# A fused two-layer network on one core: single-precision products made from half-precision parts

## The reference

```python
attn_out = out @ Wo + bo
x = x + attn_out
x_norm2 = layer_norm(x, g2, beta2)
ffn = jax.nn.relu(x_norm2 @ W1 + b1) @ W2 + b2     # W1 256 x 1024, W2 1024 x 256
return x + ffn
```

## Time and profile before

| | us |
|---|---|
| median of 3 runs | 1931.04 (1930.85 to 1933.86) |
| the profiled execution | 1943.5 |
| its span, first to last instruction | 1941.8 |
| PE busy | 1676.4 (86%) |
| VectorE busy | 1316.1 (68%) |
| ScalarE busy | 1083.6 (56%) |
| mean granted clock of PE, share of 2.4 GHz | 0.921 |

### The profile page before, as it was taken

How to read it: one execution, slowest core, us unless ns; L and a number is a source line. 1 busy time by engine, 2 the same in 40 slices (tenths; PEclk the granted TensorE clock), 3 DMA queues, 4 the chain that set the end, 5 groups by cost and what they waited for, 6 DMA issues and landing times.

```text
span 1941.8 us, 34714 instructions
## 1 busy us (share of the span) xinstructions
PE 1676.4 (86%) x13900; PEld 913.9 (47%) x13900; DVE 1316.1 (68%) x2014; ACT 1083.6 (56%) x1942; POOL 276.1 (14%) x248
## 2 busy tenths in 40 slices
PE   6988868999798999846999999999999679886877
PEld 4556645666566888521333333333333433462252
DVE  4223343381276888659999999999991686427867
ACT  3312112888643888311999999999999106311620
POOL 3223001898320000300000000000000000000000
PEclk9989989999888999875999999999999779886978
DMA  8123110899723766266433533543400070118100
GB/s 321 66 87 94 32 44 20 279 282 298 228 96 107 240 237 200 69 100 93 84 60 74 99 65 63 91 84 60 83 25 2 19 98 3 44 35 106 39 1 22
DMA packets 144653, 196.62 MB, mean 101 GB/s; under 512 B 34454, under 2 KB 109864, under 8 KB 140232
## 3 DMA queue, kind: packets, MB, share of 16 engines
q1 hardware_dynamic: 142764, 190.07, 38.1%
q0 software_dynamic: 1728, 4.33, 0.7%
HBM read 143.04 MB, written 51.00 MB: 100 GB/s over the span
## 4 chain that ended last, share of the span: by engine, by line
PE 43%; DVE 41%; issue 5%; POOL 4%; DMA 3%; ACT 2%; SPq 1%; another core or an unknown queue 1%; DVEq 0%; ACTq 0%; POOLq 0%
DVE mx_part L2200 28%; PE bank L1192 5%; PE pair L1234 5%; DVE mx L2309 3%; POOL k_part L2541 2%; PE bank L1045 2%; PE bank L1336 2%; PE pair L1395 2%; PE bank L252 2%; PE pair L1160 2%; PE pair L1147 2%; PE bank L1089 2%; DMA xT<-x_slots 2%; POOL c_lo L2528 2%; PE pair L1551 2%
## 5 line engine op out<-in xcount | busy, mean ns | idle before, releaser
L1743 ACT ACTIVATE pexp_all<-bank 128x512 f32<-128x512 f32 x1024 | 551.9, 595 | 97.9 <-PE bank L1350 84.5
L2200 DVE TENSOR_REDUCE mx_part<-pair 128x2 f32<-128x1024 f32 x512 | 583.0, 1213 | 16.6 <-PE pair L1322 14.2
L1336 PE MATMUL bank<-pexp_all,vst 128*17 128x256 f32 x4096 | 321.4, 386 | 6.0 <-issue 6.0
L1322 PE MATMUL pair<-kst,qs 49*128 49x512 f16 x1024 | 210.0, 407 | 44.7 <-DVE mx_part L2200 28.0
L1350 PE MATMUL bank<-qs,kst 52*128 52x256 f16 x2048 | 203.2, 271 | 0.0
L1322 PEld LDWEIGHTS pair<-kst,qs 49*128 49x128 f16 x1024 | 50.4, 93 | 273.2 <-DVE mx_part L2200 215.0
L1350 PEld LDWEIGHTS bank<-qs,kst 52*128 52x128 f16 x2048 | 120.7, 95 | 57.0 <-ACT pexp_all L1743 18.4
L1760 ACT ACTIVATE pexp_all<-bank 128x512 f32<-128x512 f32 x128 | 67.6, 595 | 120.5 <-PE bank L1458 120.3
L1336 PEld LDWEIGHTS bank<-pexp_all,vst 128*17 128x17 f32 x4096 | 68.6, 95 | 114.7 <-issue 105.3
L1677 ACT ACTIVATE hid_f<-bank,b 128x256 f32<-128x256 f32 (+1 forms) x152 | 78.6, 519 | 51.1 <-PE bank L1192 36.0
L1234 PE MATMUL pair<-w_hi,hid_hi 128*128 128x256 f16 x368 | 101.1, 275 | 3.2 <-issue 1.8
(11 more groups left out here) (323 smaller groups left out, 3042.5 us busy)
## 6 DMA issues: line engine op xcount, KB each, us to landing
w_f<-in_w_all SPq DMA_DIRECT2D x34, 1024.0 KB, 6.2
kst<-k_scr SPq DMA_DIRECT2D x192, 128.0 KB
v_scr<-v_st SPq DMA_DIRECT2D x64, 272.0 KB, 3.3
vst<-v_scr SPq DMA_DIRECT2D x16, 1088.0 KB, 5.6
ctx_sb<-in_ctx SPq DMA_DIRECT2D x16, 1024.0 KB, 5.0
cT<-in_ctxT SPq DMA_DIRECT2D x32, 512.0 KB, 5.6
k_scr<-k_part SPq DMA_DIRECT2D x128, 128.0 KB, 3.6
x_slots<-zeros SPq DMA_DIRECT2D x1, 3840.0 KB, 21.1
```

Source lines behind the costliest of these rows:

```text
L1322: last = pe.matmul(pair[n % 2][:, e * 512:(e + 1) * 512], qs[g % NBK][rws, p, qt * P:(qt + 1) * P], kst[g % NBK][rws, p, kb * 512:(kb + 1) ...
L1336: last = pe.matmul(bank[3][32 * h:32 * h + HV, 0:S], vst[g % 2][:, c, h * HV:(h + 1) * HV], unit_exp[n % NUE][:, p * S:(p + 1) * S], start ...
L1743: act.activation(unit_exp[n % NUE], bank[SCORE_BANKS[n % 3]], ACT.Exp, scale=SCALE).then_inc(s_exp, 1)
L2200: dve.tensor_reduce(mx_part[:, :, 2 * p + qt, kb], pair[n % 2][:, :].rearrange("p (e k) -> p e k", e=2), X_AXIS, ALU.max).then_inc(s_mx, 1)
```

## The change

- The network's two weight matrices go into one tensor of 8 pieces of 512 columns, `r_f`, with a high and a low half, `r_part`. They are loaded in `self_io(sa5)` where the expert weights are loaded in `self_io(sa6)`, and the halves are made beside steps 16 to 31 of `sa5` by the code that does it for the expert weights in `sa6`.
- `turn5` writes each transposed block twice, as single precision and as its high half; VectorE subtracts for the low half (`inputs_low`).
- Each product of the network becomes three of half precision. ScalarE's Relu writes one of four slots of `h5_f` and waits for the slot; VectorE makes the two halves of it.
- The bias row is added to `x` beside `sa5`, `u` is added between the first hidden jobs in four parts, and the scale of 1024 is taken out in the Relu and in VectorE's last addition.

```diff
-            hid5 = sb("hid5", [P, HM, NTOK], F32, sc)
-            r_w1 = sb("r_w1", [P, KT, HID], F32, sc)
-            r_w2 = sb("r_w2", [P, HM, D], F32, sc)
...
-        turn5 = Turn(tok, [(xT, "L1_attn_g2", "L1_attn_beta2")])
+        turn5 = Turn(tok, [(xT, "L1_attn_g2", "L1_attn_beta2"), (x5_part[0], "L1_attn_g2", "L1_attn_beta2")])
...
                 for b in range(B):
                     max_rows(b)
+                    if b == 1 and sa.turn == 0:
+                        sp.dma_start(r_f[:, 0:KT * HID].rearrange("p (k n) -> p k n", k=KT),
+                                     a["r_w1"].rearrange("(k p) n -> p k n", p=P)).then_inc(s_wa, 16)
+                        sp.dma_start(r_f[:, KT * HID:8 * 512].rearrange("p (m n) -> p m n", m=HM),
+                                     a["r_w2"].rearrange("(k p) n -> p k n", p=P)).then_inc(s_wa, 16)
...
             self_io(sa5, self_scr[0])
-            sa5.wait(sp, "mx", SELF_RING)
-            sp.dma_start(r_w1[:, :, :], a["r_w1"].rearrange("(k p) n -> p k n", p=P)).then_inc(s_wa, 16)
-            sp.dma_start(r_w2[:, :, :], a["r_w2"].rearrange("(k p) n -> p k n", p=P)).then_inc(s_wa, 16)
...
             pe_turn(pe, turn5, tiles_ready(norm5))
-            pe.wait_ge(s_wa, 16 * 4)
+            pe.wait_ge(s_wlo, FIRST_PIECES + 8)
             job = 0
             for half in range(2):
-                turned(pe, turn5, half)
+                pe.wait_ge(s_xlo, FIRST_INPUTS + KT * (half + 1))
                 for m in range(HM):
                     if job >= 4:
                         pe.wait_ge(s_h5e, job - 3)
                     for k in range(KT):
-                        last = pe.matmul(bank[4 + job % 4], r_w1[:, k, m * P:(m + 1) * P],
-                                         xT[:, k, half * 512:(half + 1) * 512], start=(k == 0), stop=(k == KT - 1))
+                        for i, (w_, x_) in enumerate(((0, 0), (0, 1), (1, 0))):
+                            last = pe.matmul(bank[4 + job % 4], r_w1[w_][:, k, m * P:(m + 1) * P],
+                                             x5_part[x_][:, k, half * 512:(half + 1) * 512],
+                                             start=(k == 0 and i == 0), stop=(k == KT - 1 and i == 2))
                     last.then_inc(s_h5, 1)
                     job += 1
             for t in range(T):
-                pe.wait_ge(s_h5e, HM * (t // 4 + 1))
+                pe.wait_ge(s_hlo, FIRST_HIDDEN + HM * (t // 4 + 1))
                 if t >= 2:
                     pe.wait_ge(s_x, 4 * T + t - 1)
                 for m in range(HM):
-                    last = pe.matmul(bank[2 + t % 2][:, 0:D], hid5[:, m, t * P:(t + 1) * P], r_w2[:, m, :],
-                                     start=(m == 0), stop=(m == HM - 1))
+                    for i, (h_, w_) in enumerate(((0, 0), (0, 1), (1, 0))):
+                        last = pe.matmul(bank[2 + t % 2][:, 0:D], h5_part[h_][:, m, t * P:(t + 1) * P], r_w2[w_][:, m, :],
+                                         start=(m == 0 and i == 0), stop=(m == HM - 1 and i == 2))
                 last.then_inc(s_m2, 1)
...
             def self_exp(sa):
                 for n in range(2 * SELF_STEPS):
-                    if sa.turn == 1 and n >= 32 and n % 4 == 0:
-                        last_weights_high((n - 32) // 4)
+                    if n >= 32 and n % 4 == 0:
+                        tail_weights_high(sa.turn, (n - 32) // 4)
...
             for job in range(2 * HM):
-                half, m = divmod(job, HM)
                 act.wait_ge(s_h5, job + 1)
-                act.activation(hid5[:, m, half * 512:(half + 1) * 512], bank[4 + job % 4], ACT.Relu,
-                               bias=col("L1_attn_b1", m)).then_inc(s_h5e, 1)
+                if job >= 4:
+                    act.wait_ge(s_hlo, FIRST_HIDDEN + job - 3)
+                act.activation(h5_f[:, job % 4, :], bank[4 + job % 4], ACT.Relu, bias=col("L1_attn_b1", job % HM),
+                               scale=1.0 / W_SCALE).then_inc(s_h5e, 1)
...
+            def beside_second_pass(turn, n):
                 if n >= 17 and n % 2 == 1:
-                    last_weights_low((n - 17) // 2)
+                    tail_weights_low(turn, (n - 17) // 2)
                 if n in (18, 20, 22, 24):
                     i = (n - 18) // 2
                     ts = slice(2 * i, 2 * i + 2)
+                    if turn:
+                        st.link(dve.tensor_tensor(u[:, ts, :], u[:, ts, :], per_tile_rows("L1_ffn_be1", 2), ALU.add))
+                    st.link(dve.tensor_tensor(x[:, ts, :], x[:, ts, :],
+                                              per_tile_rows("L1_ffn_be2" if turn else "L1_attn_b2", 2), ALU.add))
...
             dve_norm(dve, st, norm5, u, tok, measured=True)
-            st.link(dve.tensor_tensor(x[:, :, :], x[:, :, :], u[:, :, :], ALU.add))
+            inputs_low(turn5, x5_part)
+            for job in range(2 * HM):
+                half, m = divmod(job, HM)
+                hs = slice(half * 512, (half + 1) * 512)
+                dve.wait_ge(s_h5e, job + 1)
+                st.link(dve.tensor_copy(h5_part[0][:, m, hs], h5_f[:, job % 4, :]))
+                st.settle()
+                dve.tensor_tensor(h5_part[1][:, m, hs], h5_f[:, job % 4, :], h5_part[0][:, m, hs], ALU.subtract)\
+                    .then_inc(s_hlo, 1)
+                if job in (0, 2, 4, 6):
+                    ts = slice(job, job + 2)
+                    st.link(dve.tensor_tensor(x[:, ts, :], x[:, ts, :], u[:, ts, :], ALU.add))
             st.settle()
-            st.link(dve.tensor_tensor(x[:, :, :], x[:, :, :], per_tile_rows("L1_attn_b2"), ALU.add))
-            st.settle()
             def add_mlp(t):
                 dve.wait_ge(s_m2, t + 1)
-                dve.tensor_tensor(x[:, t, :], x[:, t, :], bank[2 + t % 2][:, 0:D], ALU.add).then_inc(s_x, 1)
+                dve.scalar_tensor_tensor(out=x[:, t, :], in0=bank[2 + t % 2][:, 0:D], scalar=1.0 / W_SCALE, in1=x[:, t, :],
+                                         op0=ALU.mult, op1=ALU.add).then_inc(s_x, 1)
```

More of the change, by code:

```diff
@@ L593, in wait @@
                 eng.wait_ge(signals[what].s, self.turn * signals[what].each + n)
-        with ExitStack() as sc:
-            sa5 = SelfAttention(0, sc)
-            cosT = sb("cosT", [P, S], F32, sc)
-            sinT = sb("sinT", [P, S], F32, sc)
-            rot_a = [sb(f"rot_a{i}", [P, 512], F32, sc) for i in range(2)]
-            rot_b = [sb(f"rot_b{i}", [P, 512], F32, sc) for i in range(2)]
-        with ExitStack() as sc:
-            hid5 = sb("hid5", [P, HM, NTOK], F32, sc)
-            r_w1 = sb("r_w1", [P, KT, HID], F32, sc)
-            r_w2 = sb("r_w2", [P, HM, D], F32, sc)
+        with ExitStack() as weights:
+            r_f = sb("r_f", [P, 8 * 512], F32, weights)
+            r_part = [sb(f"r_{part}", [P, 8 * 512], F16, weights) for part in ("hi", "lo")]
+            with ExitStack() as sc:
+                sa5 = SelfAttention(0, sc)
+                cosT = sb("cosT", [P, S], F32, sc)
+                sinT = sb("sinT", [P, S], F32, sc)
+                rot_a = [sb(f"rot_a{i}", [P, 512], F32, sc) for i in range(2)]
+                rot_b = [sb(f"rot_b{i}", [P, 512], F32, sc) for i in range(2)]
+            with ExitStack() as sc:
+                h5_f = sb("h5_f", [P, 4, 512], F32, sc)
+                h5_part = [sb(f"h5_{part}", [P, HM, NTOK], F16, sc) for part in ("hi", "lo")]
+                x5_part = [sb(f"x5_{part}", [P, KT, NTOK], F16, sc) for part in ("hi", "lo")]
+        r_w1 = [w[:, 0:KT * HID].rearrange("p (k n) -> p k n", k=KT) for w in r_part]
+        r_w2 = [w[:, KT * HID:8 * 512].rearrange("p (m n) -> p m n", m=HM) for w in r_part]
         norm4a, norm4b, norm5 = Norm(), Norm(), Norm()
@@ L617, in build @@
             wg_l = sb("wg_l", [P, KT, ER], F32, sc)
[L618 to L619 removed]
+            l_f = sb("l_f", [P, 8 * 512], F32, sc)
+            l_8 = [sb(f"l_{part}", [P, 8 * 512], F16, sc) for part in ("hi", "lo")]
+            l_part = [w[:, :].rearrange("p (e k n) -> p e k n", e=ER // 2, k=KT) for w in l_8]
             x6_part = [sb(f"x6_{part}", [P, KT, NTOK], F16, sc) for part in ("hi", "lo")]
@@ L1745, in _, with tail_weights_high @@
             act_turn(act, turn3o)
-            def last_weights_high(i):
-                act.wait_ge(s_wa, 16 * 5)
-                e, k = divmod(i, KT)
-                act.activation(l_part[0][:, e, k, :], l_we[:, e, k, :], ACT.Copy, scale=W_SCALE).then_inc(s_whi, 1)
+            def tail_weights_high(turn, i):
+                act.wait_ge(s_wa, 16 * (5 if turn else 4))
+                f, hi = ((r_f, r_part[0]), (l_f, l_8[0]))[turn]
+                cs = slice(i * 512, (i + 1) * 512)
+                act.activation(hi[:, cs], f[:, cs], ACT.Copy, scale=W_SCALE).then_inc(s_whi, 1)
             def self_exp(sa):
                 for n in range(2 * SELF_STEPS):
-                    if sa.turn == 1 and n >= 32 and n % 4 == 0:
-                        last_weights_high((n - 32) // 4)
```

(25 more changed lines are left out.)

26 lines of the change are left out of this document (13 added, 13 removed).

## The result

The change makes the kernel faster. Median 1917.24 us (6 runs, 1905.37 to 1923.24), the kernel before 1931.51 us, timed beside it (6 runs, 1930.85 to 1933.86): ratio 0.9921, 95% interval 0.9894 to 0.9947. That is 14.3 us less, where 9.6 were forecast; 1917.24 lies 0.6 us under the forecast's range. The forecast is a ratio of 0.995, just outside this interval. All three lie on the same side of it, but by the times alone the miss is small; what shows it is the profiles, stage by stage.

The account below looks back on a forecast made before the run. The prediction took PE's unbroken chain through the two-layer network as the bound. Network -11.2 us and splitting +1.6 gave -9.6, from the median of 1931.04 to 1921.4 us; range 1917.8 to 1925.5.

Parts of the forecast that it names:

- The first layer: Network's first layer: 96 half-precision products replace 32 of single precision, 22.8 us instead of 28.38, partly at half clock.
- Its start: Transposes ahead of the first layer: two destinations per job make its products start 1.0 us later, at 1674.0.
- The second layer: Network's second layer: 192 half-precision products replace 64 of single precision, 20.97 us instead of 27.64.
- VectorE and ScalarE: Under the first layer: their work stays hidden, VectorE ending about 2 us after the layer, with 3 us of cover.
- The splitting: Second pass of the self-attention ahead of the network: making the weight halves costs 1.6 us, ends 0.8 and 2.4.
- the stage ends at 1717.8, where it ended at 1729.03: 11.2 us less: End of the network's second layer: 1696.8 plus 21.0 gives 1717.8, 11.2 us less, carried whole into the sum.
- The sum: Whole kernel: -11.2 + 1.6 = -9.6 us, from the median of 1931.04 to 1921.4.
- The range: Whole kernel: 1917.8 to 1925.5 us, with the first rival in it.
- VectorE as the bound: First rival, network: at 1.45 us per pair VectorE would be late by 3 us, for 1924.4; chance 0.05.
- Late weights: Second rival, attention ahead: loads land late and hold ScalarE's first cast; at 33 us landing 1930, no change; chance 0.04.
- the cover of 15 us: Attention ahead: weights in by 1613.5, next maxima rows issued at about 1615, first cast at 1629; moved loads cost nothing.
- The clock held down: Third rival, first layer: clock stays at 1.2 GHz, layer 41.0 us, kernel 8.6 us slower, 1939.6; chance 0.04.

Follow-up runs that it names:

- after_again: The changed kernel, unchanged, timed and profiled a second time: 1933.76 us against 1949.5 for the kernel before, ratio 0.9926.
- vector_extra: The changed kernel with the cast of each hidden job made twice on VectorE: PE waits 2.67 us, the network is 4.5 us longer.
- high_only: The changed kernel with only the product of the two high halves in both layers: network 30.6 us from first product to end of last.
- before: The kernel before the change, in its first profile: profiled execution 1943.5 us, median 1931.51 us.
- before_again: The kernel before, unchanged, timed against itself and profiled a second time: 1948.79 us against 1949.5, ratio 0.9995.
- split_only: The changed kernel's loads and splitting, but the network in single precision from the loaded weights as before: ratio 0.9999 to the kernel before.
- after_shift6: The changed kernel with six small products (1.3 us) ahead of the second layer: 333.9 us from the second pass of `sa5` to the end, against 327.2.
- after: The changed kernel in its first profile: profiled execution 1923.24 us, median 1917.24 us, ratio 0.9921 to the kernel before.
- after_third: The changed kernel, unchanged, timed and profiled a third time: 1938.17 us against 1949.57 for the kernel before, ratio 0.9931.
- late_load: The changed kernel with its two weight loads issued after the fourth batch's maxima rows instead of the second's: the pass takes 64.4 us instead of 50.5.
- before_shift11: The kernel before with eleven small products (2.35 us) between the layers: 341.13 us from `sa5`'s second pass to the end, 341.10 and 341.14 without.
- the two warmed ones: Both kernels with small products on PE ahead of three norms' transposes: changed 1931.82 us beside 1949.5 (0.9905), before 1924.44 beside 1929.06 (0.9977).

## Why the forecast was wrong, point by point

The direction and the main term were right. The time lay outside the range, by 0.6 us, because the step that adds up the stages took those behind the network as fixed, and one of them got shorter; a second, smaller part is the term of the splitting, which was too large.

**The first layer**: right. 22.77 us (22.8), products 0.215 us apart, the clock rising 4.2 us after the first (4.3). The reason given, holes in the transposes that keep the clock down longer, fits the profiles: here the clock falls 0.9 to 1.8 us ahead of the first transpose in both kernels, and half speed lasts 6.8 us in the four profiles with single precision and one destination and 10.2 us in the seven with two. The agreement to 0.03 us is partly luck: in after_again the layer took 22.42 us, since the clock had fallen 0.7 us earlier against the work.

**Its start**: right, 1.1 us later (1.0). **The second layer**: right, 20.97 us (20.97). **VectorE and ScalarE**: right. VectorE ended 1.9 us after the first layer (2), and vector_extra and high_only put the point of waiting and its size where the count had them. The network as a whole gave 11.4 us, forecast 11.2.

**The splitting**: the mechanism was right and the size was not. The step "from the exponentials at 1629.22 to the gathering ... from the cast at 1818.45" measured one stretch from the exponentials and the other from the cast ahead of them. That cast lies in idle time, so its 0.6 us were wrongly counted as cost; read from the same event the rows give 1.06. By the profiles it is 1.0 us to the gathering (1.6 forecast, ends 0.8 to 2.4). To the network's transposes it is 0.4 on average; that last 0.6 is where the clock falls in the pass and in the projection behind it, and no size of the splitting.

**What was missing**: "the stage ends at 1717.8, where it ended at 1729.03: 11.2 us less" took for granted that all behind it keeps its length. The same work behind the network runs 3.4 or 10.2 us at half speed, by where the fall of the clock lies against PE's transposes. The table has all profiles without added products ahead of the norm, worked out from windows of 0.2 us:

| profile | the clock falls, us ahead of the first transpose | half speed lasts | projection |
|---|---|---|---|
| before | 0.96 | 10.2 | 9.61 |
| before_again | 0.84 | 10.2 | 9.67 |
| split_only | 1.67 | 10.2 | 9.26 |
| after_shift6 | 1.73 | 10.2 | 9.23 |
| vector_extra | 1.10 | 10.2 | 9.54 |
| after | 0.03 | 3.4 | 7.34 |
| after_again | 0.38 | 3.4 | 7.34 |
| after_third | 0.03 | 3.4 | 7.34 |
| high_only | 0.31 | 3.4 | 7.34 |
| late_load | 0.14 | 3.4 | 7.34 |
| before_shift11 | 0.10 inside them | 3.4 | 7.34 |

The fall itself comes 3 to 4.8 us after PE's last product of the network. PE then stands idle up to the transposes; between them and the projection it idles another 0.7 us. In the kernel before the clock had fallen 0.96 us ahead of the transposes and came back only in the projection. In the changed one it fell 0.03 us ahead of them and came back at 1719.77, inside the last transposes. That gave 2.3 us in the projection and 2.5 with the transposes. The remaining 0.3 of the 2.8 us up to the maxima is not clock but the balance of two others: SyncE's ten issues of that chain took 1.4 us less (one of 1.86 us is now 0.45), and the last read took 1.1 us more to land; the short issues come in the kernel before too, in before_shift11. The forecast used this very row of the kernel before to size the clock in the first layer, and did not ask what would become of that row itself. The two shifted kernels and the two warmed ones show it from both sides. The further 0.8 us less up to the gathering of `sa6` and 0.7 more in the tail cancel. They go with the clock too: where the former takes 72.4 us (after, after_third) the clock comes back to full 26.0 to 26.4 us after the first maxima, and where it takes 73.5 to 73.6 (before, before_again, after_again) 29.0 to 29.3 us after them. What sets this, no run tested.

**The sum**: 0.4 - 11.4 - 2.8 - 0.8 + 0.7 = -13.9 us, against -9.6. Of the 4.3 us, 2.8 lie behind the network (2.5 the clock, 0.3 issues and landings), 1.2 in the stretch with the splitting (0.6 its size, 0.6 the clock), 0.2 in the network, the rest in the later stages.

**The range** was built from the terms of the edited stages, each with its own ends, and from 3 us of scatter between runs. It had no term for stages that keep their code and change their place against the clock. The rule of the Trainium skill on swings of the clock by short stops (TensorE: Matmul & The Clock Gate, A second HAM failure mode: psum-queue depth-cycling) does not show in the first layer: the granted clock is 1.00 from 1672 to 1690 us, with four banks in turn. What the Trainium skill says of transposes (same page, Part 4: PE-mode transpose), that they do not count as busy time for the clock, is contradicted again: in the changed kernel the clock rises at 1719.77 us, and PE had nothing but transposes, from 1716.39 on, since the network's end at 1711.7.

**The rivals**: VectorE as the bound (1924.4) did not come, and 7.2 us more of work on it cost 4.5. Late weights did not come, and the cover of 15 us was real: with the loads issued 27 us later the wait is 11.0, so 16 were covered. The clock held down did not come.

## What to carry to other kernels

When a stage gets shorter or longer, ask of each idle time and each burst of PE behind it where the granted clock will now change, for one or two stages on: here that was nearly a fifth of the gain (2.5 of 13.9 us), and 2.35 us of added work were free by the same effect. Price an edit that exists elsewhere in the kernel from the same event to the same event in both places. A stop of PE costs more than its length where the clock falls with it: 2.67 us of waiting cost 4.5 here, and 11.0 cost 13.9.

## What the runs showed of the hardware that I had not expected

The same program took 1931.5, 1949.5, 1929.1 and 1949.6 us (medians of before) in four sets of runs: two levels 18 to 20 us apart, so only ratios within a set mean anything. Within a set the executions of the kernel before spread by 3 us in one and by 9 to 18 in the others, those of the changed one by 9 to 18 in all three of theirs. Some 10 of the 18 to 20 us sit in one stage that nobody changed, the last shared expert: its hidden products take 31 to 32 us in all profiles of the two sets at 1949 us, and 20.7 in all of the set at 1929 us. ScalarE waits there for something that the profile does not name; the rest of the distance stays open.

With nothing but transposes on PE the clock came up after 3.4 us, ahead of their end, where it had fallen at most 0.4 us before them. Where it had fallen 0.8 us or more before them (five profiles), a hole of 0.7 us between the transposes and the next products followed, and half speed lasted 10.2 us. No run separates the idle time ahead of the transposes from the hole behind them.
